# A new order of the instruction lists in the layer unit of a fused selective-scan kernel, and the product of steps 12 and 13 wholly on GpSimd

## The reference, cut to what matters

```python
def mamba_layer(x, p):                       # H=192, I=384, N=16 states, R=48, K=4
    h = rmsnorm(x, nw)
    u, z = split(einsum('blh,ch->blc', h, in_w))
    u = silu(causal_conv(u, cw, cb))
    proj = einsum('bli,ci->blc', u, xp_w)
    dt_r, Bm, Cm = proj[..., :R], proj[..., R:R+N], proj[..., R+N:]
    dt = softplus(einsum('blr,ir->bli', dt_r, dtw) + dtb)
    # scan over tokens: h = exp(dt * A) * h + (dt * u) * B ;  y = sum over N of h * C
    y = selective_scan(u, dt, -exp(a_log), Bm, Cm, D)
    y = y * silu(z)
    return x + einsum('bli,hi->blh', y, ow)
```

## Time and profile before

| what | value |
|---|---|
| median of 3 runs | 13553.63 us (13551.23 to 13554.96) |
| profiled execution, its own time | 13543.7 us |
| its span in the trace | 13541.9 us |
| VectorE busy | 12672.3 us, 94% |
| GpSimd busy | 12133.6 us, 90% |
| TensorE matmul busy | 11900.2 us, 88% |
| ScalarE busy | 11185.8 us, 83% |
| mean of all transfers | 155 GB/s |

### The profile page before, as it was taken

How to read it: one execution, slowest core, us unless ns; L and a number is a source line. 1 busy time by engine, 2 the same in 40 slices (tenths; PEclk the granted TensorE clock), 3 DMA queues, 4 the chain that set the end, 5 groups by cost and what they waited for, 6 DMA issues and landing times. The chain is left out here.

```text
span 13541.9 us, 201184 instructions
## 1 busy us (share of the span) xinstructions
PE 11900.2 (88%) x53560; PEld 6601.2 (49%) x53560; DVE 12672.3 (94%) x7562; ACT 11185.8 (83%) x23486; POOL 12133.6 (90%) x3795
## 2 busy tenths in 40 slices
PE   7888888888888888888888888888888888888899
PEld 5444444444444444444444444444444444444776
DVE  4999999999999999999999999999999999999543
ACT  4888888888888888888888888888888888888311
POOL 3999999999999999999999999999999999999034
PEclk8999999999999999999999999999999999999889
DMA  4555555555555555555555555555555555555123
GB/s 130 161 165 162 165 162 161 167 161 170 165 166 162 163 162 162 167 160 167 162 167 166 165 165 161 166 159 166 161 166 161 162 168 163 169 164 157 48 58 72
DMA packets 794394, 2099.99 MB, mean 155 GB/s; under 512 B 97604, under 2 KB 382340, under 8 KB 791552
## 3 DMA queue, kind: packets, MB, share of 16 engines
q1 hardware_dynamic: 697072, 1688.67, 35.6%
q0 software_dynamic: 95808, 403.86, 15.2%
q10 hardware_dynamic: 720, 0.55, 0.0%
HBM read 1419.25 MB, written 288.23 MB: 126 GB/s over the span
## 5 line engine op out<-in xcount | busy, mean ns | idle before, releaser
L990 POOL TENSOR_TENSOR dbu<-dtu_rep,b_rep 128x1944 f32<-128x1944 f32 x2056 | 9132.4, 4510 | 148.5 <-DMA dtu_rep<-dtu_rows 101.6
L925 DVE TENSOR_TENSOR_SCAN h<-ps,dbu 128x972 f32<-128x972 f32 x4109 | 8707.3, 2165 | 178.1 <-ACT ps L701 159.2
L701 ACT ACTIVATE ps<-dt_rep,A_cur 128x323 f32<-128x323 f32 x12327 | 5906.1, 522 | 901.2 <-DVE h L925 808.8
L519 PE MATMUL ps<-h,fold 128*32 128x486 f32 x16408 | 3454.8, 588 | 130.4 <-POOL h L999 119.6
L933 DVE TENSOR_TENSOR h<-h,ps 128x1944 f32<-128x1944 f32 (+2 forms) x2052 | 3455.9, 1695 | 3.0 <-PE ps L506 3.0
L999 POOL TENSOR_TENSOR h<-h,c_rep 128x972 f32<-128x972 f32 (+1 forms) x769 | 2239.6, 2975 | 8.4 <-DVE h L925 4.8
L603 PE MATMUL ps<-u_raw,w_cv 128*128 128x162 f32 (+7 forms) x8256 | 1802.2, 371 | 19.1 <-ACT terms L745 10.5
L603 PEld LDWEIGHTS ps<-u_raw,w_cv 128*128 128x128 f32 x8256 | 1360.0, 190 | 491.9 <-ACT terms L745 149.3
L519 PEld LDWEIGHTS ps<-h,fold 128*32 128x32 f32 x16408 | 754.2, 110 | 1628.7 <-issue 1345.2
L590 PE MATMUL ps<-x_norm,w_u 96*128 96x324 f32 (+1 forms) x4144 | 995.4, 384 | 243.0 <-ACT x_R L732 178.5
L506 PE MATMUL ps<-xp_rows,sel_c 16*128 16x324 f32 x2052 | 830.1, 484 | 332.1 <-DVE h L933 320.9
(11 more groups left out here) (189 smaller groups left out, 11608.0 us busy)
## 6 DMA issues: line engine op xcount, KB each, us to landing
dt_rep<-dt_rows SPq DMA_DIRECT2D x1028, 486.0 KB, 6.4
dtu_rep<-dtu_rows SPq DMA_DIRECT2D x1028, 486.0 KB, 6.0
sums<-terms POOLq DMA_DIRECT2D x258, 972.0 KB, 6.7
b_rep<-b_rows SPq DMA_DIRECT2D x1029, 162.0 KB, 5.8
sums<-sums POOLq DMA_DIRECT2D x258, 486.0 KB, 4.5
dtu_rows<-terms SPq DMA_DIRECT2D x258, 486.0 KB, 2.8
dt_rows<-sums SPq DMA_DIRECT2D x257, 486.0 KB, 3.5
c_rep<-b_rows SPq DMA_DIRECT2D x771, 162.0 KB, 2.8
```

The source lines that it names most:

```text
L519: mm = pe.matmul(y_ps[32 * r:32 * r + 32, half, :], fold[:, :], flat(h, step)[:, half * YW:(half + 1) * YW], start=(s < NR), stop=(s == la ...
L701: ins = act.activation(decay[s % 2][:, it * L + 1:(it + 1) * L], dt_rep[:, s % NR, it, 1:L], ACT.Exp, scale=A_cur[:, it * N + s:it * N + s ...
L925: dve.tensor_tensor_scan(flat(h, s), decay[s % 2], flat(dbu, s), 0.0, ALU.mult, ALU.add).then_inc(s_scan, 1)
L990: pool.tensor_tensor(steps(dbu, s, 2), steps(dtu_rep, r, 2), each(b_rep[:, q, :], 2), ALU.mult).then_inc(s_dbu, 1)
```

## The change

Two things change. `SHARED` becomes empty and 12 leaves `PRODUCTS`: GpSimd multiplies the whole of steps 12 and 13 (128 x 1944), and VectorE's instruction of 128 x 324 is gone. And the lists of all five engines in the layer unit get a new order; every other instruction and transfer stays, with its size, operands and semaphores. VectorE's list, written flat (s = scan, p = product, A and B the units; single products are p2 and p6), becomes

The store of dt moves from the head of SP's step to its end, B's quarter 2 is loaded one step of the loop earlier, and in the layer's last units the reload of `w_cv` comes between the second and the third load of the step. The changed lines, without the unchanged ones between them:

```diff
@@ -320,17 +320,17 @@
-EXPS = (0, 1, 2, 3, 4, 5, 6, 7, 8, 9, 11, 10, 13, 12, 15, 14)
-SCANS = (0, 1, 2, 3, 4, 5, 6, 7, 9, 8, 11, 10, 13, 12, 14, 15)
+EXPS = (0, 1, 2, 3, 4, 5, 6, 7, 8, 9, 10, 11, 12, 13, 14, 15)
+SCANS = (0, 1, 2, 3, 4, 5, 6, 7, 8, 9, 10, 11, 12, 13, 14, 15)
...
-PRODUCTS = (0, 2, 4, 6, 8, 10, 12, 14)
+PRODUCTS = (0, 2, 4, 6, 8, 10, 14)
...
-SUMS = (0, 2, 4, 6, 8, 10, 12, 14)
+SUMS = (0, 4, 2, 6, 8, 10, 12, 14)
...
-SHARED = {12: 5}
+SHARED = {}
...
@@ -639,47 +639,46 @@
+    if on[2]:
+        freed = te_conv(pe, v[2], 0, freed)
...
-        freed = te_conv(pe, v[2], 0, freed)
+        freed = te_conv(pe, v[2], 1, freed)
...
+        te_sum(pe, v[0], 6)
...
-        freed = te_conv(pe, v[2], 1, freed)
+        freed = te_xp(pe, v[2], q[2], freed)
...
-        te_sum(pe, v[0], 6)
...
-        freed = te_xp(pe, v[2], q[2], freed)
...
-    if on[1]:
-        te_bcast(pe, v[1], q[1], 0)
+    if on[0]:
+        te_sum(pe, v[0], 12)
...
-        te_sum(pe, v[0], 12)
+        te_sum(pe, v[0], 14)
...
-    if on[0]:
-        te_sum(pe, v[0], 14)
+    if on[1]:
+        te_bcast(pe, v[1], q[1], 0)
...
-        te_bcast(pe, v[1], q[1], 1)
+        te_sum(pe, v[1], 0)
...
-    if on[1]:
-        te_sum(pe, v[1], 0)
...
-        te_sum(pe, v[1], 2)
+        te_bcast(pe, v[1], q[1], 1)
...
@@ -688,6 +687,8 @@
+    if on[1]:
+        te_sum(pe, v[1], 2)
@@ -838,81 +839,79 @@
+        se_decay(act, v[0], 9)
+    if on[2]:
+        se_ur(act, v[2], 1)
+    if on[0]:
+        se_decay(act, v[0], 10)
+        se_decay(act, v[0], 11)
...
-        se_decay(act, v[0], 15)
-        se_decay(act, v[0], 14)
+        se_decay(act, v[0], 13)
...
+        se_copy_cb(act, v[2])
...
+        se_silu_u(act, v[2], q[2])
+    act.preload_act_table_set(MAIN_SET)
+    if on[0]:
+        se_decay(act, v[0], 14)
+        se_decay(act, v[0], 15)
...
-        se_silu_u(act, v[2], q[2])
-    act.preload_act_table_set(MAIN_SET)
+        se_xp(act, v[2], q[2])
...
-        se_xp(act, v[2], q[2])
+        se_dt(act, v[2], 0)
...
-    if on[2]:
-        se_dt(act, v[2], 0)
-    if on[1]:
-        se_decay(act, v[1], 2)
...
+    if on[1]:
+        se_decay(act, v[1], 2)
...
+    if on[2]:
+        se_one_plus(act, v[2])
...
-        se_one_plus(act, v[2])
-        se_log(act, v[2])
-        se_lost(act, v[2])
...
-        se_less(act, v[2])
...
+        se_log(act, v[2])
...
-    if on[1]:
-        se_decay(act, v[1], 5)
+        se_lost(act, v[2])
+        se_less(act, v[2])
...
+        se_decay(act, v[1], 5)
...
-        se_decay(act, v[1], 7)
-        se_decay(act, v[1], 8)
...
-        se_decay(act, v[1], 9)
+        se_decay(act, v[1], 7)
...
-    if on[3]:
-        se_copy_cb(act, v[3])
-    if on[1]:
-        se_decay(act, v[1], 11)
+        se_copy_nw(act, v[4])
+        se_log_ss(act, v[4])
+    if on[1]:
+        se_decay(act, v[1], 8)
+    if on[4]:
+        se_rstd(act, v[4])
...
-    if on[1]:
-        se_decay(act, v[1], 10)
-    if on[4]:
-        se_log_ss(act, v[4])
-        se_copy_nw(act, v[4])
-        se_rstd(act, v[4])
-    if on[3]:
-        se_ur(act, v[3], 1)
-    if on[1]:
-        se_decay(act, v[1], 13)
...
@@ -945,36 +944,33 @@
+        ve_scan(dve, v[0], 9)
+        ve_scan(dve, v[0], 10)
+        ve_scan(dve, v[0], 11)
...
+        ve_product(dve, v[0], 6)
+        ve_scan(dve, v[0], 13)
...
-        ve_product(dve, v[0], 12)
+        ve_product(dve, v[0], 14)
...
-    if on[0]:
-        ve_product(dve, v[0], 14)
-    if on[1]:
...
+    if on[0]:
+        ve_gate(dve, v[0], q[0])
+    if on[1]:
...
-    if on[0]:
-        ve_gate(dve, v[0], q[0])
-    if on[1]:
+        ve_scan(dve, v[1], 4)
...
-        ve_scan(dve, v[1], 4)
...
+        ve_product(dve, v[1], 4)
...
-        ve_product(dve, v[1], 4)
-        ve_scan(dve, v[1], 9)
...
-        ve_scan(dve, v[1], 11)
-        ve_product(dve, v[1], 6)
-        ve_scan(dve, v[1], 10)
-        ve_scan(dve, v[1], 13)
@@ -1025,6 +1021,7 @@
+        ge_dbu(pool, v[0], 14)
...
@@ -1035,16 +1032,14 @@
-        ge_product(pool, v[1], 3)
+        ge_dbu(pool, v[1], 10)
...
-        ge_dbu(pool, v[1], 10)
+        ge_product(pool, v[1], 3)
+        ge_dbu(pool, v[1], 12)
...
-    if on[1]:
-        ge_dbu(pool, v[1], 12)
-        ge_dbu(pool, v[1], 14)
@@ -1159,40 +1154,39 @@
-        sp_store_dt(sp, v[1])
-    if "u" in due:
-        reload_u(sp, u + 2)
+        sp_load_dt(sp, v[1], 0)
...
-        sp_load_dtu(sp, v[1], 0)
...
-        sp_load_b(sp, v[1], q[1], 2)
-        sp_load_dtu(sp, v[1], 3)
-        sp_load_b(sp, v[1], q[1], 3)
-        sp_load_dt(sp, v[1], 0)
-        sp_load_dt(sp, v[1], 3)
-        sp_load_dtu(sp, v[1], 2)
-        sp_load_b(sp, v[1], q[1], 1)
-        sp_load_dt(sp, v[1], 2)
-        sp_load_c(sp, v[1], q[1], 1)
...
+    if on[1]:
+        sp_load_dtu(sp, v[1], 0)
+        sp_load_dtu(sp, v[1], 3)
+        sp_load_dtu(sp, v[1], 2)
+        sp_load_b(sp, v[1], q[1], 3)
+        sp_load_c(sp, v[1], q[1], 0)
+        sp_load_dt(sp, v[1], 2)
+        sp_load_b(sp, v[1], q[1], 1)
+        sp_load_dt(sp, v[1], 3)
+        sp_load_c(sp, v[1], q[1], 2)
+        sp_load_c(sp, v[1], q[1], 1)
...
+    if "u" in due:
+        reload_u(sp, u + 3)
...
-    if on[2]:
-        sp_load_b(sp, v[2], q[2], 0)
-    if on[1]:
-        sp_load_c(sp, v[1], q[1], 0)
-        sp_load_c(sp, v[1], q[1], 2)
...
+        sp_store_dt(sp, v[2])
+        sp_load_b(sp, v[2], q[2], 2)
+        sp_load_b(sp, v[2], q[2], 0)
...
@@ -1226,17 +1220,17 @@
-            sync_step(sp, first + B - 4, 0)
-            sync_step(sp, first + B - 3, 1, due=('u', 'c', 'x', 'z'))
+            sync_step(sp, first + B - 4, 0, due=('u',))
+            sync_step(sp, first + B - 3, 1, due=('c', 'x', 'z'))
...
-        for s, ahead in zip(s_bq + s_cr, (3, 2, 2, 2, 2, 2, 2)):
+        for s, ahead in zip(s_bq + s_cr, (3, 2, 3, 2, 2, 2, 2)):
...
-        sp.wait_ge(s_dst[0], 16 * (UNITS + 2))
+        sp.wait_ge(s_dst[0], 16 * (UNITS + 3))
```

More of the change, by code:

```diff
@@ L863, in scalar_step @@
             if on[2]:
-                se_dt(act, v[2], 0)
+                se_dt(act, v[2], 1)
+                se_exp_x(act, v[2])
             if on[1]:
                 se_decay(act, v[1], 2)
-            if on[2]:
-                se_dt(act, v[2], 1)
-                se_exp_x(act, v[2])
             if on[3]:
                 se_x_norm(act, v[3], q[3], 0)
+            if on[2]:
+                se_one_plus(act, v[2])
             if on[1]:
@@ L952, in vector_step @@
                 ve_scan(dve, v[0], 15)
-                ve_product(dve, v[0], 12)
+                ve_product(dve, v[0], 14)
             if on[1]:
                 ve_scan(dve, v[1], 0)
-            if on[0]:
-                ve_product(dve, v[0], 14)
-            if on[1]:
                 ve_scan(dve, v[1], 1)
                 ve_scan(dve, v[1], 2)
-                ve_product(dve, v[1], 0)
-                ve_scan(dve, v[1], 3)
             if on[0]:
@@ L965, in vector_step @@
             if on[1]:
+                ve_product(dve, v[1], 0)
+                ve_scan(dve, v[1], 3)
+                ve_scan(dve, v[1], 4)
                 ve_product(dve, v[1], 2)
-                ve_scan(dve, v[1], 4)
                 ve_scan(dve, v[1], 5)
                 ve_scan(dve, v[1], 6)
+                ve_product(dve, v[1], 4)
                 ve_scan(dve, v[1], 7)
-                ve_product(dve, v[1], 4)
-                ve_scan(dve, v[1], 9)
                 ve_scan(dve, v[1], 8)
-                ve_scan(dve, v[1], 11)
-                ve_product(dve, v[1], 6)
-                ve_scan(dve, v[1], 10)
-                ve_scan(dve, v[1], 13)
         def ge_dbu(pool, u, s):
```

## The result

The changed kernel takes **13472.5 us** (median of 4 runs, 13469.8 to 13473.9) against 13552.4 for the kernel before, measured beside it: ratio 0.9942, 95% interval 0.9926 to 0.9958. It is 80 us faster, where 182 were forecast. The sign was right and the time lies in the range of 13290 to 13520, but less than half of the gain came. The profiled execution has a span of 13472.1 us, so 69.8 us less than before: 69.8 / 256 = 0.27 us a unit, where the sum said 0.71. So 0.44 us a unit is missing.

What follows compares the result with a forecast made beforehand. VectorE's list was taken to bound: 47.34 us a unit less 0.47, plus 0.25 of waits, gives 47.12 against 47.83. Saving 0.71 x 256 = 182 us put the median at 13372 us, range 13290 to 13520.

Steps and rivals of the forecast that it cites:

- What bounds, and the removed third: VectorE's list sets the layer unit's period; removing its 128 x 324 instruction takes off all 0.47 us, 47.34 to 46.87.
- The order itself costs nothing if no item is late: VectorE's new list, laid out from fixed times per scan and product, adds nothing: scan 9 returns at 46.9 us.
- The residual waits, 0.25 us a unit: VectorE's waits remaining in the new order, taken between none and the earlier 0.49 us a unit.
- the tight places: Four points on VectorE: p8 (spare 0.7 us), p0 and s10 (0.2 to 0.3 each), and s0, which needs dbu 0.
- The transfers: Room from dt * u to dbu 0 shrinks from 14.36 to 10.80 us, leaving 6.6 for a load; costed at nothing.
- The 21 us for `w_cv`: Once in 15 layers reload_c delays the second dtu load: 1.4 x 15 = 21 us, 0.08 a unit, within the 0.25.
- The spare of 1.3 us at `dbu` 0: GpSimd finishes dbu 0 at about 20.5 against s0 at 21.9, so a single late one up to 1.3 us costs nothing.
- Rival 1: GpSimd becomes the bound: 46.52 us plus the 0.93 pause before its first accumulating transfer, 47.45 a unit, 13457 us; chance 0.15.
- Rival 2: TensorE's clock falls in gaps before out0 and u0, costing 0.33 us a unit: period 47.45, 13457 us; chance 0.10.
- Rival 3: New waits add up to what was saved, 0.96 us a unit, leaving 13554 us; chance 0.08.
- The two chains with 0.25 us to spare: Chains into VectorE's p0 and s10, each with 0.2 to 0.3 us spare; no gain if both run half a microsecond longer.
- Rival 4: Loads of dt * u land too late for GpSimd, at 8.3 us: 100 us slower, 13654 us; chance 0.09.

Runs made afterwards that it cites:

- rotate_late_c: Changed kernel with SP's loop over layers cut after a step's last load and the w_cv reload put behind the step's loads: 13376.0 us, ratio 0.9872.
- late_c: Changed kernel with only the reload of w_cv put behind all loads of its step: 13449.8 us, ratio 0.9934.
- order_alone: Changed kernel's new order of all lists, but the third of pair 12, 13 back on VectorE: 13540.6 us, ratio 0.9992 to the kernel before.
- split14: As rotate_late_c, with VectorE's product of steps 14 and 15 made by two instructions of 128 x 972: 13332.9 us, ratio 0.9838.
- rotate: Changed kernel with only SP's loop over layers cut after the last load of a step, transfer order unchanged: 13410.7 us, ratio 0.9902.

## Why the prediction was right in its sign and wrong in its size

- **What bounds, and the removed third.** Right for the new order. VectorE's list bounds there, and the third is worth 68 us (13540.6 to 13472.5), about 0.47 less the 0.18 that it had hidden, 0.29 x 256 = 74. That "all of it comes off" does not hold in the old order, where the same move cost 19 us.
- **"The order itself costs nothing if no item is late."** This step failed. I took each instruction's distance from its start to the next as fixed. It is longer when the next one waits for what it wrote: product 14 behind scan 15, 0.18 us, which the sum put at nothing. That is 0.18 x 256 = 46 us of the missing gain; taking it away gave back 43 and 42 us in two kernels.
- **The residual waits, 0.25 us a unit.** This term failed too, by half: the missing 0.44 less 0.18 leaves 0.26, so they were about 0.51. Their kind was wrong too. I looked for them in the tight places of an ordinary unit, and those held: ScalarE's waits fell from 195 to 29, and `rotate_late_c` shows some 15 us of named waits in 11000. They sit at the layer's end, in "The transfers". The 21 us for `w_cv` were about right (`late_c` gave 23, not clear of noise). But I passed over SP's jump, a standstill of 4 us in the same room that the new order shortened. Cutting the loop elsewhere gave back 62 us, both edits 96 us.
- **The spare of 1.3 us at `dbu` 0** was right for an ordinary unit: `dbu` 0 is done at about 6127.5 (6123.24 + 4.27), and scan 0 starts at 6128.71. VectorE's 27 waits for `dbu` in 231 units are beyond it. But a late load costs VectorE more than the first wait, 5.2 us in all behind one of 2.1.
- **Rival 1, GpSimd bounds** (0.15): no, by `order_alone` and `split14`. The pause of 0.93 us is ScalarE being late. The Trainium skill, "GPSIMD Engine Reference", section 4.1 "Engine selection", has its factor of two borne out (4.27 against 2.07 us). The trade of 0.71 us for 0.47 was still worth making, but only in an order that leaves GpSimd that room.
- **Rival 2, the clock** (0.10): no. The mean of an `xp` matmul fell from 562 to 453 ns, and TensorE no longer waits before it (230.9 us of waits in 11000 before, none after). ScalarE still waits before it evicts `xp`, 115 times, but for 30.1 us in all instead of 84.5. At `out` and `u`, where the loss was to come, the means stayed (327 to 326 and 381 to 381 ns). The mean granted clock of the whole rose from 0.965 to 0.979.
- **Rival 3, no change** (0.08): no, the interval of the ratio ends at 0.9958. The two chains with 0.25 us to spare, on which it rests, held in ordinary units.
- **Rival 4, late loads** (0.09): the mechanism is there, but at two places of a layer and not in each unit, and the larger of the two, the jump, was not named.

With the layer's end mended the time is 13376, and with product 14 split 13333, 1.6% under the kernel before.

## What to carry to other kernels

Two changes to a full schedule are not the sum of their parts: the order alone gave 9 us, the move alone lost 19, both together gained 80 (the 9 is not clear of noise). As the timelines have it, the short instruction that was removed was also what one engine did while another finished a chain. When an order shortens the room of a transfer, look at the rarest unit, not the median one: the loop's jump, the reloads, whatever happens once in sixteen. And a start-to-start distance holds only for a pair whose second does not read the first; here a product right behind its own scan started 0.18 us later.

## What the runs showed of the hardware that was not expected

SP stood still for about 4 us at each jump back of its outer loop. Between 1000 and 12000 us there are 15 jumps; the next transfer follows the store of dt * u by 4.43 to 4.47 us at all of them, against 0.5 us in a unit without a jump (7146.49 to 7151.07 in the old list: 4.55 to 4.62, against 0.57). With the loop cut elsewhere the pause moved with it: `b_rows` is then stored 6.6 to 7.9 us after the start of the last pair of loads, instead of 1.6 to 2.8. The jump of the inner loop, over two units, shows too: 1.1 us instead of 0.5 in the changed kernel, and 0.5 to 0.6 in `rotate`. The loads of dt * u were no later for it, and none of the 29 waits stands there.

```profile
6354.92 1.26 SPq L1067 DMA_DIRECT2D c_rep<-b_rows  x2
6357.00 0.33 SPq L1051 DMA_DIRECT2D b_rows<-xp_rows  x1
```

That is an ordinary unit of `rotate_late_c`; the one at the jump:

```profile
6307.87 1.21 SPq L1067 DMA_DIRECT2D c_rep<-b_rows  x2
6314.85 0.34 SPq L1051 DMA_DIRECT2D b_rows<-xp_rows  x1
```

Every kernel with the old order moved 6.1 MB in 741 to 745 packets through its instruction queue, every one with the new order 0.87 to 0.89 MB in 106 to 110. The profile lists 201184 instructions in the kernel before and 200925 in the changed one, so they are about equally long. Which engine's code that is, and whether it cost the old order time, is open.
